# Moebius and attention rounds: the order in which the groups of tiles join and leave

## The chip, the cores and the metric

One core of a Trainium2 chip runs the whole program. The metric is the device time of one execution in microseconds (us); "before" is the median of three runs. A profiled execution is a little longer than these and gives the trace.

## The reference, cut to what matters

Four graph layers run one after the other on 6250 nodes with 128 features and 106250 edges (100000 random ones and a loop on every node): a SAGE layer with two convolutions, a Moebius (hyperbolic) aggregation, an equivariant convolution, and a graph attention. The change lies in the second and the fourth, and in how both order the nodes.

The Moebius layer folds a node's messages one after the other, because `mobius_add` isn't associative:

```python
messages = mobius_add(x[src], -x[dst])
def body(out, em):
    m, idx = em
    return (out.at[idx].set(mobius_add(out[idx], m)), None)
total, _ = jax.lax.scan(body, out0, (messages, dst))
```

The attention layer takes for each node a softmax over its incoming edges, per head, of `leaky_relu(a_src + a_dst + a_edge)`, and the weighted sum of the sources' projected rows; then come a bias and two layer norms with a residual.

## The kernel before, in words

The 6250 nodes stand in 49 tiles of 128, sorted by falling degree (in-edges), so that tile 0 holds the nodes with the most edges. The ranks are worked out on VectorE in the second SAGE sweep (function of that stage, step `k == PLACED`, line 1270), and the rows of the nodes are scattered to HBM in that order.

In the Moebius and the attention stage every partition holds one node of a tile, and each round gives every active tile one more edge. A *half-turn* is one such round; a *turn* is two (`r` = 0, 1), with two halves of the buffer `rows`, so that the gathers of one half-turn run beside the arithmetic of the other. The tiles are in eight groups of `SIZES = (1, 4, 4, 8, 10, 9, 7, 6)`; group 0 is the tile of highest degree. All 49 tiles start together, and the groups leave from the last to the first when their largest degree is used up: `phases` (line 1470) gives, for p = 7 down to 0, the turns in which the groups 0 to p are active. `plan_span` (line 1402) works out the numbers of turns on VectorE from the degrees and writes them to `turns`; all engines load them into registers (`turn_counts`, `turns_before`) and loop over them (`Fori`). Every phase has a loop body of its own in the code of each engine.

A half-turn in the Moebius stage:

- POOL issues one indirect gather per active tile (L1585), 128 rows of `x1_tab` into `rows`. It waits for the indices (`idx_ready`), and before each group until ScalarE has read that group's rows of two half-turns ago (`scaled_ready`).
- ScalarE copies each chunk of up to four tiles to PSUM when its group has landed (L1622), makes the indices of two half-turns later (L1624), waits for the factors `gm` (L1784) and scales each tile's rows (L1633).
- VectorE multiplies each chunk (L1744) and adds it up (L1736), runs some 40 small operations on one number per node (L1755, the mask of nodes with edges left, to L1794), and folds each tile (L1799). When all turns are done it plans the next span (L1434, L1435 and on, L1405 to L1424).

A half-turn in the attention stage: POOL gathers (L2535) when the run of ten tiles has been consumed two half-turns ago; ScalarE makes indices (L2598) and exponentials (L2602); VectorE makes the mask (L2633), the scores (L2636 to L2645), and for each run rescales, weights and adds (L2662, L2665, L2654). When a group of the last five has left, `finish` (L2681 to L2739 on VectorE, with square roots and normalisations on ScalarE) makes the output rows of its tiles; group 3 and the joint groups 0 to 2 are finished together at the end. POOL scatters the output (L2520), 49 in all: 32 after the last gather, then it waits for all engines, SyncE clears the semaphores, POOL reloads a span (L1449, L2545, L1455), and the last 17 scatters follow.

The lines that say in which order tiles are worked on:

```python
PART = tuple(slice(UPTO[g] - SIZES[g], UPTO[g]) for g in range(NG))
def phases(turns):
    for p in reversed(range(NG)):
        yield p, turns[p + 1] if p + 1 < NG else 0, turns[p]
...
        FINISH = [(g, 0, PART[g]) for g in range(NG - 1, 2, -1)] + [(0, 1, slice(0, UPTO[2]))]
        INSIDE = NG - 4
```

## Time and profile before

| | us |
|---|---|
| time before, median of 3 runs | 6176.32 (6172.39 to 6184.4) |
| profiled execution, its own time | 6204.05 |
| its span | 6202.3 |
| POOL busy | 4463.9 (72%) |
| VectorE (DVE) busy | 3342.5 (54%) |
| Moebius rounds, first gather to the plan | 2409.7 to 3616.5 |
| attention, first gather to the end of the span | 4981.0 to 6202.3 |

Times in the trace count from the start of the span. "Busy" is the time in which an engine runs instructions; a row of a group of instructions has the line, the engine, the operation, what it writes and reads, the count, busy us, mean ns of one, and then the engine's idle time just before them with what ended it. "Issue" there is idle time for which the profile shows no wait.

### The profile page before, as it was taken

Reading aid. Unit: us, or ns where it says so; the run is one execution under the profiler, and the core shown is the slowest. Engines: PE = TensorE matmul, PEld = TensorE weight load, DVE = VectorE, ACT = ScalarE, POOL = GpSimd, SP = SyncE. Lnnn points to the kernel's source line nnn. Section 1 sums busy time; section 2 is a strip of 40 time slices with the busy share of each in tenths; the row PEclk is TensorE's granted clock in tenths of the full one; section 3 lists DMA queues with packets and bytes.
Section 4 is the critical chain, followed back from the end, with each engine's and each line's share of the span. In section 5 each row is a group of like instructions: output and inputs, shape, how many; then the busy total and the mean of one; then the engine's idle time right before and its main releaser. Section 6 shows DMA issues by size and latency. Waiting matters only on the chain. (4 is left out here: it accounts for less than half of the span.)

```text
span 6202.3 us, 54339 instructions
## 1 busy us (share of the span) xinstructions
PE 2518.5 (41%) x12736; PEld 1802.9 (29%) x12736; DVE 3342.5 (54%) x8895; ACT 1718.2 (28%) x5753; POOL 4463.9 (72%) x4570
## 2 busy tenths in 40 slices
PE   6888877567776673000000024656666400000000
PEld 4666656455544452000000012334444300000000
DVE  3333333433444355878778875655555524343666
ACT  1111111211111110333333256777777400000111
POOL 6777777577777766777777437777777777777775
PEclk8777676777899875555555567888788755555555
DMA  4333333866666633222222114333333332222221
GB/s 113 119 116 119 116 118 114 208 210 189 191 188 187 179 94 95 54 54 54 54 54 54 34 47 115 101 112 111 110 111 112 105 98 56 55 56 56 56 53 41
DMA packets 404899, 637.29 MB, mean 103 GB/s; under 512 B 148580, under 2 KB 248966, under 8 KB 404340
## 3 DMA queue, kind: packets, MB, share of 16 engines
q0 software_dynamic: 175664, 424.09, 24.4%
q1 hardware_dynamic: 133028, 112.92, 6.7%
q10 hardware_dynamic: 95904, 96.94, 4.8%
q8 instruction: 105, 1.72, 0.1%
q14 instruction: 198, 1.62, 0.1%
HBM read 529.65 MB, written 103.93 MB: 102 GB/s over the span
## 5 line engine op out<-in xcount | busy, mean ns | idle before, releaser
L1585 POOL DMA_INDIRECT mb_rows<-x_tab,mb_idx x882 | 835.5, 947 | 367.2 <-issue 269.8
L2535 POOL DMA_INDIRECT gt_rows<-h_tab,gt_idx x882 | 842.1, 955 | 307.1 <-issue 273.9
L973 POOL DMA_INDIRECT s_rows<-y_split,srcS x824 | 839.3, 1019 | 292.9 <-issue 233.1
L2035 POOL DMA_INDIRECT eq_ring<-fx_tab,srcS x824 | 834.4, 1013 | 262.3 <-issue 248.2
L555 POOL DMA_INDIRECT s_rows<-in_x,srcS x824 | 784.2, 952 | 273.7 <-issue 247.7
L2070 ACT ACTIVATE eq_ring<-eq_ring 128x64 f32<-128x64 f32 x3328 | 814.5, 333 | 338.6 <-DVE eq_ring L2231 310.7
L2111 PE MATMUL eq_ps<-eq_ring,eq_onehot 128*128 128x320 f32 x1664 | 655.6, 552 | 473.5 <-DVE eq_ring L2231 253.0
L2111 PEld LDWEIGHTS eq_ps<-eq_ring,eq_onehot 128*128 128x128 f32 x1664 | 385.3, 242 | 720.3 <-issue 658.6
L1054 PE MATMUL s_ps<-s_onehot,s_rows 128*128 128x128 bf16 x4992 | 452.0, 247 | 310.0 <-DMA s_rows<-y_split,srcS 300.8
L1695 PE MATMUL mb_ps<-ident,mb_rows 128*128 128x128 f32 x49 | 13.6, 331 | 1282.6 <-ACT mb_rows L1662 1281.3
L629 PE MATMUL s_ps<-s_onehot,s_rows 128*128 128x128 f32 x1664 | 459.7, 393 | 159.6 <-DMA s_rows<-in_x,srcS 152.8
L1054 PEld LDWEIGHTS s_ps<-s_onehot,s_rows 128*128 128x128 bf16 x4992 | 355.7, 112 | 431.5 <-DMA s_rows<-y_split,srcS 394.4
L194 DVE TENSOR_TENSOR s_onehot<-iota,dstM 128x512 bf16<-128x512 f32 x206 | 143.2, 696 | 600.6 <-PE s_ps L1054 599.8
L629 PEld LDWEIGHTS s_ps<-s_onehot,s_rows 128*128 128x128 f32 x1664 | 352.5, 254 | 268.8 <-DMA s_rows<-in_x,srcS 215.3
L1744 DVE TENSOR_TENSOR mb_prod<-mb_ps,mb_xf 128x256 f32<-128x256 f32 (+3 forms) x278 | 274.7, 996 | 209.5 <-ACT mb_ps L1622 177.0
L1695 PEld LDWEIGHTS mb_ps<-ident,mb_rows 128*128 128x128 f32 x49 | 6.8, 145 | 1289.9 <-issue 1280.3
L2228 DVE TENSOR_TENSOR eq_ring<-eq_ring 128x512 f32<-128x512 f32 x208 | 143.6, 691 | 439.4 <-DMA eq_ring<-fx_tab,srcS 428.6
L1633 ACT ACTIVATE mb_ps<-mb_rows,mb_gm 128x128 f32<-128x128 f32 x882 | 260.1, 351 | 324.0 <-DVE mb_gm L1784 324.0
L194 DVE TENSOR_TENSOR s_onehot<-s_ps,dstM 128x512 f32<-128x512 f32 x206 | 142.3, 691 | 289.9 <-PE s_ps L630 289.8
L2636 DVE TENSOR_TENSOR span_src<-gt_rows,edges_in 128x196 f32<-128x196 f32 (+7 forms) x36 | 9.4, 261 | 505.7 <-DMA gt_rows<-h_tab,gt_idx 504.4
L1736 DVE TENSOR_REDUCE mb_both<-mb_prod 128x2 f32<-128x256 f32 (+3 forms) x278 | 272.6, 988 | 0.3
L1622 ACT COPY mb_ps<-mb_rows 128x128 f32<-128x128 f32 (+3 forms) x278 | 128.0, 494 | 494.1 <-DMA mb_rows<-x_tab,mb_idx 449.8
(503 smaller groups left out, 5693.9 us busy)
## 6 DMA issues: line engine op xcount, KB each, us to landing
w_tab<-s_wrow ACTq DMA_DIRECT2D x208, 264.0 KB
eq_ring<-w_tab SPq DMA_DIRECT2D x208, 264.0 KB, 2.7
s_es<-in_side ACTq DMA_DIRECT2D x208, 136.0 KB
mb_rows<-x_tab,mb_idx POOLq DMA_INDIRECT x882, 2.5
gt_rows<-h_tab,gt_idx POOLq DMA_INDIRECT x882, 2.5
s_rows<-in_x,srcS POOLq DMA_INDIRECT x824
s_rows<-y_split,srcS POOLq DMA_INDIRECT x824
eq_ring<-fx_tab,srcS POOLq DMA_INDIRECT x824
```

Source lines behind the costliest of these rows:

```text
L194: return dve.tensor_tensor(onehot[:, 4 * half:4 * half + 4], broadcast(numbers, four, 1), broadcast(columns, four, 2), ALU.is_equal)
L555: pool.indirect_dma_start(rows[:, n % SLOTS, :], None, a["x"], bass.IndirectOffsetOnAxis(ap=s["srcS"][:, n:n + 1], axis=0)).then_inc(gathe ...
L629: pe.matmul(ps[:, bank, 0:P], rows[:, slot], onehot[:, u], start=(u == 0), stop=(u == U - 1))
L973: pool.indirect_dma_start(rows[:, n % SLOTS, :], None, t["ys"], bass.IndirectOffsetOnAxis(ap=s["srcS"][:, n:n + 1], axis=0)).then_inc(gath ...
L1054: last = pe.matmul(ps[:, 2 * bank + f, 0:P], rows[:, slot, at:at + P], onehot[:, u], start=(u == 0 and part == 0), stop=(u == U - 1 and pa ...
L1585: pool.indirect_dma_start(rows[:, r, n, :], None, t["x1"], bass.IndirectOffsetOnAxis(ap=idx[:, r, n:n + 1], axis=0)).then_inc(gathered[r][ ...
L1736: do.put(dve.tensor_reduce(both[:, :, lo:hi], prod[:, c % 3, :, 0:hi - lo], AX_X, ALU.add))
L1744: dve.tensor_tensor(prod[:, c % 3, :, 0:hi - lo], copied(c).unsqueeze(1).broadcast_to(wide), xf[:, :, lo:hi, 0:D], ALU.mult).then_inc(mult ...
L2035: pool.indirect_dma_start(frow[:, n % SLOTS, :], None, features, bass.IndirectOffsetOnAxis(ap=s["srcS"][:, n:n + 1], axis=0)).then_inc(gat ...
L2070: last = act.activation(pb[:, r % 2, u, f].rearrange("p c w -> p (c w)"), wrow[:, r, u, lo:lo + 64], ACT.Copy, scale=wrow[:, r, u, D + f:D ...
L2111: last = pe.matmul(ps[:, bank, 0:MC], onehot[:, 4 * h + u], msg[:, h, u], start=(h == 0 and u == 0), stop=(h == 1 and u == 3))
L2535: pool.indirect_dma_start(rows[:, r, n, :], None, flat, bass.IndirectOffsetOnAxis(ap=idx[:, r, n:n + 1], axis=0)).then_inc(gathered[r][g], 16)
```

## The change

The tiles are laid out anew: the 27 tiles of groups 0 to 4 stand in rising order of degree (group 4 first, group 0 last), then groups 5, 6, 7. The ranks get three more operations that reverse the first 27 x 128. The rounds begin with groups 0 to 4 alone. When group 4 (ten tiles) has ended, groups 5, 6 and 7 (22 tiles) join with their first edges, and the groups leave in the order 4, 3, 2, 1, 7, 6, 5, 0. So the active tiles are always adjacent (`WINDOW`). Because the joined groups count their turns from the joining, masks, index columns and semaphore values use two counts, `e` and `e + turns[0]` (`group_turn`), and operations on a column of edges are made once for each of up to two windows. In the attention stage the runs of ten tiles become six unequal stretches, every group is finished when it leaves, and 48 of the 49 scatters come ahead of the reload.

```diff
 WTILES = 2 * BODIES * WB
 NT = TILES + 1
 SPAN = 48
+SRCS = SPAN + 15
 READY = tuple(-(-(G * P * (g + 1) * E // N + 700) // EB) for g in range(GROUPS - 1))
 SIZES = (1, 4, 4, 8, 10, 9, 7, 6)
 NG = len(SIZES)
-UPTO = tuple(sum(SIZES[:g + 1]) for g in range(NG))
-PART = tuple(slice(UPTO[g] - SIZES[g], UPTO[g]) for g in range(NG))
-CHUNKS = tuple((g, n, min(n + 4, UPTO[g])) for g in range(NG) for n in range(PART[g].start, PART[g].stop, 4))
-CHUNKS_TO = tuple(sum(1 for c in CHUNKS if c[0] <= g) for g in range(NG))
+FIRST = 5
+PLACES = (*reversed(range(FIRST)), *range(FIRST, NG))
+PART = tuple(slice(sum(SIZES[x] for x in PLACES[:PLACES.index(g)]), sum(SIZES[x] for x in PLACES[:PLACES.index(g) + 1]))
+             for g in range(NG))
+HEAD = PART[FIRST].start
+LEAVE = (4, 3, 2, 1, 7, 6, 5, 0)
+TURN = (0, 5, 6, 7, 1, 2, 3, 4)
+ACTIVE = tuple(tuple(g for g in TURN if LEAVE.index(g) >= p and (p or g < FIRST)) for p in range(NG))
+WINDOW = tuple((min(PART[g].start for g in on), max(PART[g].stop for g in on)) for on in ACTIVE)
+CHUNKS = tuple((g, n, min(n + 4, PART[g].stop)) for g in TURN for n in range(PART[g].start, PART[g].stop, 4))
+CHUNKS_TO = {g: max(k for k, c in enumerate(CHUNKS) if c[0] == g) + 1 for g in range(NG)}
+ON = tuple(tuple(k for k, c in enumerate(CHUNKS) if c[0] in on) for on in ACTIVE)
 WW = D + 4
...
                 if k == PLACED:
+                    do(dve.tensor_scalar(key, rank[:], -2.0, float(HEAD * P - 1), ALU.mult, ALU.add))
+                    do(dve.scalar_tensor_tensor(key, rank[:], float(HEAD * P), key, ALU.is_lt, ALU.mult))
+                    do(dve.tensor_tensor(rank[:], rank[:], key, ALU.add))
                     do(dve.tensor_copy(s["rank"][:], rank[:]))
...
-    for g in range(NG):
-        do.put(dve.tensor_reduce(q[:, 0, g:g + 1], s["tile_max"][:, PART[g]], AX_X, ALU.max))
+    for j, g in enumerate(LEAVE):
+        do.put(dve.tensor_reduce(q[:, 0, j:j + 1], s["tile_max"][:, PART[g]], AX_X, ALU.max))
     do.sync()
...
-    for g in range(NG - 2, -1, -1):
-        do(dve.scalar_tensor_tensor(q[:, 1, g:g + 1], q[:, 1, g + 1:g + 2], 1.0, q[:, 1, g:g + 1], ALU.add, ALU.max))
+    do(dve.tensor_scalar(q[:, 1, 4:7], q[:, 1, 4:7], q[:, 1, 0:1], None, ALU.add))
+    for j in range(1, NG):
+        do(dve.scalar_tensor_tensor(q[:, 1, j:j + 1], q[:, 1, j - 1:j], 1.0, q[:, 1, j:j + 1], ALU.add, ALU.max))
     do(dve.tensor_tensor(q[:, 2, 0:NG], q[:, 2, 0:NG], q[:, 3, 0:NG], ALU.add))
     do.put(dve.tensor_copy(s["turns"][:, 1, 0:NG], q[:, 2, 0:NG]))
     do.put(dve.tensor_copy(s["turns"][:, 0, 0:NG], q[:, 1, 0:NG]))
     do(dve.tensor_copy(q[:, 3, 0:NG], q[:, 1, 0:NG]))
-
-
-PLAN_OPS = 5 + NG + 6 + (NG - 1) + 4
+    do.put(dve.tensor_scalar(q[:, 3, 4:7], q[:, 1, 4:7], q[:, 1, 0:1], None, ALU.subtract))
+    do(dve.tensor_scalar(s["turns"][:, 0, 1:NG], q[:, 1, 1:NG], q[:, 1, 0:1], None, ALU.subtract))
+
+
+PLAN_OPS = 5 + NG + 7 + (NG - 1) + 6
...
 def phases(turns):
-    for p in reversed(range(NG)):
-        yield p, turns[p + 1] if p + 1 < NG else 0, turns[p]
+    for p in range(NG):
+        yield p, turns[p - 1] if p > 1 else 0, turns[p]
 
 
 def turn_counts(eng, s):
 
-    return [eng.value_load(s["turns"][0:1, 0, g:g + 1], min_val=1, max_val=SPAN // 2 + NG - 1) for g in range(NG)]
+    return [eng.value_load(s["turns"][0:1, 0, p:p + 1], min_val=1, max_val=SPAN // 2 + NG - 1) for p in range(NG)]
 
 
 def turns_before(eng, s):
 
-    return [eng.value_load(s["turns"][0:1, 1, g:g + 1], min_val=0, max_val=65535 // (16 * SIZES[g]) - 2 * SPAN) for g in range(NG)]
+    return [eng.value_load(s["turns"][0:1, 1, LEAVE.index(g):LEAVE.index(g) + 1], min_val=0,
+                           max_val=65535 // (16 * SIZES[g]) - 2 * SPAN) for g in range(NG)]
+
+
+def group_turn(p, g, e, turns):
+    return e + turns[0] if p and g < FIRST else e
+
+
+def windows(p):
+    lo, hi = WINDOW[p]
+    return [(0, lo, HEAD)] if hi <= HEAD else [(0, lo, HEAD), (FIRST, HEAD, hi)]
+
+
+def source_column(s, lo, hi, k):
+    return s["span_all"][:, bass.ds(k + lo * SRCS, (hi - lo) * SRCS)].rearrange("p (t k) -> p t k", k=SRCS)[:, :, 0]
 
...
             with pool.Fori(0, span_count(pool, s)) as c:
-                for p, lo, hi in phases(turn_counts(pool, s)):
-                    with pool.Fori(lo, hi) as b:
+                turns = turn_counts(pool, s)
+                for p, lo, hi in phases(turns):
+                    with pool.Fori(lo, hi) as e:
+                        b = group_turn(p, 0, e, turns)
                         for r in range(2):
                             pool.wait_ge(idx_ready[r], b + 1)
                             pool.sem_inc(took, 1)
-                            for g in range(p + 1):
+                            for g in ACTIVE[p]:
...
+                                act.copy(copied(i, hi_ - lo_), rows[:, r, lo_:hi_, 0:D]).then_inc(copied_ready, after(p, i) - k)
+                            for first, lo_, hi_ in windows(p):
+                                ins = act.copy(idx[:, r, lo_:hi_],
+                                               source_column(s, lo_, hi_, group_turn(p, first, e, turns) * 2 + (2 + r)))
+                            ins.then_inc(idx_ready[r], 1)
...
-                            for k in range(CHUNKS_TO[p]):
+                            for i, k in enumerate(ON[p]):
                                 g, lo_, hi_ = CHUNKS[k]
-                                if k >= 4:
...
-            def turn(p, b, r):
-                T = UPTO[p]
-                many = CHUNKS_TO[p]
+            def turn(turns, p, e, b, r):
+                at, to = WINDOW[p]
+                T, many = to - at, len(ON[p])
                 dve.sem_clear(own)
...
                         dve.wait_ge(own, c - 2)
                     wide = [P, 2, hi - lo, D]
-                    dve.tensor_tensor(prod[:, c % 3, :, 0:hi - lo], copied(c).unsqueeze(1).broadcast_to(wide), xf[:, :, lo:hi, 0:D],
...
-                xs2, y2 = rows[:, r, 0:T, D], xd[:, 0:T, D]
-                dve.tensor_scalar(valid, s["span_deg"][:, 0:T], s["iota"][:, bass.ds(2 * b + r, 1)], None, ALU.is_gt)
...
+                xs2, y2 = rows[:, r, at:to, D], xd[:, at:to, D]
+                for first, lo, hi in windows(p):
+                    dve.tensor_scalar(w[5][:, lo:hi], s["span_deg"][:, lo:hi],
+                                      s["iota"][:, bass.ds(group_turn(p, first, e, turns) * 2 + r, 1)], None, ALU.is_gt)
                 dve.tensor_scalar(t0, dt, -2.0, 1.0, ALU.mult, ALU.add)
...
-        column = lambda T, k, f: edges_in[:, bass.ds(k, T * SPAN)].rearrange("p (t j) f -> p t j f", j=SPAN)[:, :, 0, f]
+        column = lambda lo, hi, k, f: edges_in[:, bass.ds(k + lo * SPAN, (hi - lo) * SPAN)].rearrange(
+            "p (t j) f -> p t j f", j=SPAN)[:, :, 0, f]
         bias, gain, shift = (sb(n, [P, D]) for n in ("bias", "gain", "shift"))
         idx = sb("idx", [P, 2, TILES], I32)
         MOST = max(SIZES)
-        RUN = 10
-        RUNS = -(-TILES // RUN)
-        FINISH = [(g, 0, PART[g]) for g in range(NG - 1, 2, -1)] + [(0, 1, slice(0, UPTO[2]))]
-        INSIDE = NG - 4
+        STRETCHES = ((26, 36), (36, 43), (43, 49), (18, 26), (10, 18), (0, 10))
+        RUNS = len(STRETCHES)
+        run_of = lambda n: next(c for c, (lo, hi) in enumerate(STRETCHES) if lo <= n < hi)
+        own_run = lambda p, c, e, turns: group_turn(p, 0 if STRETCHES[c][0] < HEAD else FIRST, e, turns)
+        runs_of = lambda p: [(c, max(lo, WINDOW[p][0]), min(hi, WINDOW[p][1])) for c, (lo, hi) in enumerate(STRETCHES)
+                             if lo < WINDOW[p][1] and hi > WINDOW[p][0]]
+        FINISH = [(g, 0, PART[g]) for g in LEAVE]
         stats, mv = sb("stats", [P, 2, MOST, 6]), sb("mv", [P, 2, MOST, 2])
...
                         for r in range(2):
                             pool.wait_ge(idx_ready[r], b + 1)
                             pool.sem_inc(took, 1)
-                            for g in range(p + 1):
+                            opened = set()
+                            for g in ACTIVE[p]:
                                 for n in range(PART[g].start, PART[g].stop):
-                                    if n % RUN == 0:
-                                        pool.wait_ge(consumed[r][n // RUN], b + 1)
+                                    if run_of(n) not in opened:
+                                        opened.add(run_of(n))
+                                        pool.wait_ge(consumed[r][run_of(n)], own_run(p, run_of(n), e, turns) + 1)
                                         pool.sem_inc(took, 1)
                                     pool.indirect_dma_start(rows[:, r, n, :], None, flat,
                                                             bass.IndirectOffsetOnAxis(ap=idx[:, r, n:n + 1], axis=0)
                                                             ).then_inc(gathered[r][g], 16)
-                for k in range(INSIDE):
+                for k in range(NG - 1):
                     pool.wait_ge(normed[0], 2 * k + 2)
                     scatter(FINISH[k][2])
...
                 pool.sem_inc(src_ready, 1)
-                for k in range(INSIDE, len(FINISH)):
-                    scatter(FINISH[k][2])
+                scatter(FINISH[NG - 1][2])
                 pool.wait_ge(scattered, 16 * TILES)
...
+                    with dve.Fori(lo, hi) as e:
+                        b = group_turn(p, 0, e, turns)
                         for r in range(2):
-                            turn(before, p, b, r)
-                    if NG - 1 - p < INSIDE:
-                        finish(NG - 1 - p)
-                finish(INSIDE, INSIDE + 1)
+                            turn(turns, before, p, e, b, r)
+                    finish(p)
```

## Rows read from the trace of the kernel before

**Rows 1.** Page, part 1, and POOL's busy tenths of 40 slices (part 2)

```profile
PE 2518.5 (41%) x12736; PEld 1802.9 (29%) x12736; DVE 3342.5 (54%) x8895; ACT 1718.2 (28%) x5753; POOL 4463.9 (72%) x4570
...
POOL 6777777577777766777777437777777777777775
```

**Rows 2.** Page, part 5 (Moebius gathers) and part 6 (attention's, us to landing)

```profile
L1585 POOL DMA_INDIRECT mb_rows<-x_tab,mb_idx x882 | 835.5, 947 | 367.2 <-issue 269.8
...
gt_rows<-h_tab,gt_idx POOLq DMA_INDIRECT x882, 2.5
```

**Rows 3.** Waits of the Moebius stage: us in total, times, longest

```profile
POOL mb_rows L1585 <- ACT mb_ps L1633: 70.8, 22, 9.3
...
POOL mb_rows L1585 <- ACT mb_idx L1624: 26.6, 5, 7.4
...
DVE mb_prod L1744 <- issue: 24.2, 5, 5.0
```

**Rows 4.** Timeline of the Moebius stage, first gather and planning

```profile
2409.68 0.99 POOL L1585 DMA_INDIRECT mb_rows<-x_tab,mb_idx  x1 [9.38 <-issue]
...
3616.52 0.15 DVE L1434 TENSOR_SCALAR base<-base 128x1 f32<-128x1 f32 x1 [0.32 <-DVE mb_xf L1799]
```

**Rows 5.** Groups of VectorE's instructions by shape, Moebius stage, line L1755

```profile
L1755 DVE TENSOR_SCALAR mb_w<-span_deg,iota 128x49 f32<-128x49 f32 x12 | 3.0, 249 | 1.9 <-DVE mb_both L1736 1.9
...
L1755 DVE TENSOR_SCALAR mb_w<-span_deg,iota 128x1 f32<-128x1 f32 x10 | 2.1, 214 | 1.6 <-DVE mb_both L1736 1.6
...
L1755 DVE TENSOR_SCALAR mb_w<-span_deg,iota 128x5 f32<-128x5 f32 x4 | 1.1, 282 | 0.6 <-DVE mb_both L1736 0.6
...
L1755 DVE TENSOR_SCALAR mb_w<-span_deg,iota 128x43 f32<-128x43 f32 x2 | 0.5, 244 | 0.3 <-DVE mb_both L1736 0.3
```

**Rows 6.** Windows from mask to mask, Moebius: length, busy PE, PEld, DVE, ACT, POOL

```profile
2539.02:2600.26 61.24, 0.00 (x0) 0.00 (x0) 48.62 (x117) 21.68 (x65) 46.30 (x50) 0.50 0.21 55
...
3386.84:3420.60 33.76, 0.00 (x0) 0.00 (x0) 28.72 (x82) 11.88 (x36) 25.53 (x28) 0.50 0.21 55
...
3445.18:3466.22 21.04, 0.00 (x0) 0.00 (x0) 19.75 (x66) 7.52 (x23) 15.13 (x16) 0.50 0.21 55
...
3466.22:3483.01 16.79, 0.00 (x0) 0.00 (x0) 15.17 (x61) 6.41 (x21) 8.51 (x9) 0.50 0.13 33
...
3483.01:3496.82 13.81, 0.00 (x0) 0.00 (x0) 12.52 (x54) 4.07 (x13) 4.74 (x5) 0.50 0.12 29
...
3539.89:3548.39 8.50, 0.00 (x0) 0.00 (x0) 6.78 (x46) 1.85 (x7) 0.95 (x1) 0.50 0.04 8
...
3576.31:3583.03 6.72, 0.00 (x0) 0.00 (x0) 5.38 (x42) 0.68 (x3) 0.95 (x1) 0.50 0.01 2
```

**Rows 7.** Windows, attention: half-turn of 49 tiles, finish of 10, half-turn of 17

```profile
5628.26:5689.09 60.83, 0.00 (x0) 0.00 (x0) 24.95 (x30) 2.07 (x3) 46.07 (x49) 0.50 0.22 56
...
6005.96:6029.86 23.90, 0.00 (x0) 0.00 (x0) 19.51 (x65) 5.96 (x16) 18.11 (x20) 0.50 0.22 57
...
6042.90:6053.87 10.97, 0.00 (x0) 0.00 (x0) 9.92 (x20) 0.51 (x2) 8.32 (x9) 0.50 0.22 58
```

**Rows 8.** Waits of the attention stage, POOL's own

```profile
POOL gt_rows L2535 <- DVE gt_ps L2665: 25.4, 9, 7.3
...
POOL gt_rows L2535 <- ACT gt_idx L2598: 7.7, 3, 2.6
```

**Rows 9.** Timeline of the attention stage, its start and its end

```profile
4980.96 0.99 POOL L2535 DMA_INDIRECT gt_rows<-h_tab,gt_idx  x1 [8.92 <-issue]
...
5001.03 6.82 POOL L2535 DMA_INDIRECT gt_rows<-h_tab,gt_idx  x1 [0.30 <-issue]
...
6169.46 0.15 DVE L1424 COPY plan_q<-plan_q 1x8 f32<-1x8 f32 x1
...
6178.34 0.99 POOL L2520 DMA_INDIRECT out<-gt_rows,perm  x1 [1.05 <-issue]
...
6198.62 0.96 POOL L2520 DMA_INDIRECT out<-gt_rows,perm  x1 [0.30 <-issue]
```

More of the change, by code:

```diff
@@ L1635, in _ @@
+                                ins.then_inc(scaled_ready, after(p, i) - k)
                 act.sem_inc(arrived, 1)
@@ L1743, in turn @@
                     wide = [P, 2, hi - lo, D]
[L1744 to L1745 removed]
+                    dve.tensor_tensor(prod[:, c % 3, :, 0:hi - lo], copied(c, hi - lo).unsqueeze(1).broadcast_to(wide), xf[:, :, lo:hi, 0:D],
+                                      ALU.mult).then_inc(multiplied, after(p, c) - k)
                     if c:
@@ L1806, in _ @@
                 for p, lo, hi in phases(turns):
-                    with dve.Fori(lo, hi) as b:
+                    with dve.Fori(lo, hi) as e:
+                        b = group_turn(p, 0, e, turns)
                         for r in range(2):
-                            turn(p, b, r)
+                            turn(turns, p, e, b, r)
                 do = Chain(dve, plan_own, c * NEXT_OPS)
@@ L2524, in _ @@
             with pool.Fori(0, span_count(pool, s)) as c:
-                for p, lo, hi in phases(turn_counts(pool, s)):
-                    with pool.Fori(lo, hi) as b:
+                turns = turn_counts(pool, s)
+                for p, lo, hi in phases(turns):
+                    with pool.Fori(lo, hi) as e:
+                        b = group_turn(p, 0, e, turns)
                         for r in range(2):
@@ L2622, in _, with turn @@
             by_head = "p u (h c) -> p u h c"
-            def turn(before, p, b, r):
-                T = UPTO[p]
+            def turn(turns, before, p, e, b, r):
+                at, to = WINDOW[p]
+                T = to - at
                 four = [P, T, heads]
-                aek = column(T, 2 * b + r, slice(0, heads))
-                al, sc, dn, old, new = alpha[:, 0:T], scores[:, 0:T], den[:, 0:T], top[:, 1 - r, 0:T], top[:, r, 0:T]
-                adst = own_row[:, 0:T, D + heads:HW]
-                valid4 = valid[:, 0:T].unsqueeze(2).broadcast_to(four)
+                al, sc, dn, old, new = alpha[:, at:to], scores[:, at:to], den[:, at:to], top[:, 1 - r, at:to], top[:, r, at:to]
+                adst = own_row[:, at:to, D + heads:HW]
+                valid4 = valid[:, at:to].unsqueeze(2).broadcast_to(four)
@@ L2631, in turn @@
                 dve.sem_clear(turn_own)
                 do = Chain(dve, turn_own)
-                dve.tensor_scalar(valid[:, 0:T], s["span_deg"][:, 0:T], s["iota"][:, bass.ds(2 * b + r, 1)], None, ALU.is_gt)
-                for g in range(p + 1):
-                    dve.wait_ge(gathered[r][g], (before[g] + b + 1) * (16 * SIZES[g]))
-                do(dve.tensor_tensor(al, rows[:, r, 0:T, D:D + heads], aek, ALU.add))
-                dve.tensor_scalar(limit_[:, 0:T], valid[:, 0:T], 2.0 * BIG, -BIG, ALU.mult, ALU.add)
+                spans = windows(p)
@@ new lines, in turn @@
+                for first, lo, hi in spans:
+                    dve.tensor_scalar(valid[:, lo:hi], s["span_deg"][:, lo:hi],
+                                      s["iota"][:, bass.ds(group_turn(p, first, e, turns) * 2 + r, 1)], None, ALU.is_gt)
+                for g in ACTIVE[p]:
+                    dve.wait_ge(gathered[r][g], (group_turn(p, g, e, turns) + before[g] + 1) * (16 * SIZES[g]))
+                aek = [column(lo, hi, group_turn(p, first, e, turns) * 2 + r, slice(0, heads)) for first, lo, hi in spans]
@@ L2640, in turn @@
                 do(dve.scalar_tensor_tensor(al, al, NEG, al, ALU.mult, ALU.max))
-                do(dve.tensor_tensor(sc, al, limit_[:, 0:T].unsqueeze(2).broadcast_to(four), ALU.min))
+                do(dve.tensor_tensor(sc, al, limit_[:, at:to].unsqueeze(2).broadcast_to(four), ALU.min))
                 do(dve.tensor_tensor(new, sc, old, ALU.max))
-                dve.tensor_tensor(below[:, 0, 0:T], old, new, ALU.subtract)
-                dve.tensor_tensor(below[:, 1, 0:T], sc, new, ALU.subtract).then_inc(below_ready, 1)
@@ L2649, in turn @@
-                runs = [(c, c * RUN, min(c * RUN + RUN, T)) for c in range(-(-T // RUN))]
-                weights = lambda c, many: ps[:, 1 + 3 * (c % 2):4 + 3 * (c % 2), :].rearrange("p b n -> p (b n)")[:, 0:many * D]
-                def add_up(c, lo, hi):
-                    dve.wait_ge(consumed[r][c], b + 2)
-                    do.put(dve.tensor_tensor(acc[:, lo:hi], weights(c, hi - lo).rearrange("p (u d) -> p u d", d=D),
+                dve.tensor_tensor(dn, dn, ex[:, 0, at:to], ALU.mult)
@@ new lines, in turn, with add_up @@
+                do(dve.tensor_tensor(ex[:, 1, at:to], ex[:, 1, at:to], valid4, ALU.mult))
+                runs = [(i, c, lo, hi) for i, (c, lo, hi) in enumerate(runs_of(p))]
+                weights = lambda i, many: ps[:, 1 + 3 * (i % 2):4 + 3 * (i % 2), :].rearrange("p b n -> p (b n)")[:, 0:many * D]
+                def add_up(i, c, lo, hi):
+                    dve.wait_ge(consumed[r][c], own_run(p, c, e, turns) + 2)
+                    do.put(dve.tensor_tensor(acc[:, lo:hi], weights(i, hi - lo).rearrange("p (u d) -> p u d", d=D),
@@ L2655, in add_up @@
                                              acc[:, lo:hi], ALU.add))
-                    added[c] = do.n
+                    added[i] = do.n
                 added = {}
-                for c, lo, hi in runs:
+                for i, c, lo, hi in runs:
                     wide = [P, hi - lo, heads, cols]
```

127 lines of the change are left out of this document (65 added, 62 removed).

## The prediction

> **What bounds the kernel now.** I read the page first, then the groups of instructions with their shapes, windows cut at half-turns, the two lists of waits, and the timeline where the two stages begin and end. The reader is to see in the page that POOL is busy for 72% of the span, more than any other engine, and that its busy share falls twice while work is still left: in the 23rd and 24th slice, and in the last [rows 1]. The first dip is the tail of the Moebius stage, the second that of the attention stage. Both stages are long rows of indirect gathers, 882 each; one takes 947 ns and the engine then sits 0.305 us on "issue" (269.8 us in the 855 cases that are no other wait, 9.4 of them ahead of the first) [rows 2, 3, 4]. So a gather costs 1.252 us, and 882 of them cost 1104.3 us in each stage, however they are ordered.
>
> How the gathers are spread is in the shapes of L1755, one per half-turn: 12 half-turns on 49 tiles, two each on 43, 36, 27, 17 and 9 (the rows of 36, 27, 17 and 9 read like that of 43), four on 5 and ten on 1 [rows 5]. That is 36 half-turns, 18 turns, and says when each group ends: group 7 after 6 turns, then 7, 8, 9, 10, 11, 13 and 18 for group 0. The windows show two regimes [rows 6]. With 49 tiles a half-turn takes 61.24 us, which is 49 x 1.252 = 61.3: gathers set it, and VectorE is busy for 48.62. With 27 tiles it takes 33.76 (27 x 1.252 = 33.8), VectorE busy 28.72; with 17, 21.04 (21.3). Below that VectorE sets it: 13.81 with 9 tiles where the gathers need 11.3, 6.72 with one where they need 1.25. So POOL waits there: 70.8 + 26.6 us in 27 waits, of which 27 x 0.305 is the usual issue time, which leaves 89.2 us [rows 3]. The account closes: 2409.7 + 1104.3 + 89.2 is 3603.2, and the planning that follows the last half-turn begins at 3616.5 [rows 4].
>
> Attention is the same with less VectorE work: with 49 tiles the half-turn is 60.83 us and VectorE is busy for 24.95 [rows 7]. POOL's waits there are 25.4 + 7.7 us in 12 cases, so 29.4, and one gather takes 6.82 instead of 0.95 [rows 8, 9]; together 35.3 beyond 1104.3, so the last slot ends at 4981.0 + 1139.6 = 6120.6.
>
> **The change part by part.** *Turns.* Groups 0 to 4 (27 tiles) run first, nine turns, until group 4 ends; then groups 5, 6, 7 join with 8, 7 and 6 turns of their own and end at turns 17, 16 and 15, group 0 at 18. From the ends above the active tiles by turn are 27 (nine times), 39, 31, 27, 27, 23, 23, 17, 10, 1. Twice their sum, 441, is 882: not one gather less, and the same 36 half-turns. What moves is where they lie: only the last four half-turns (10, 10, 1, 1) are below 17 tiles, against 16 before.
>
> *Moebius.* I let POOL set every half-turn of 17 tiles or more, as the windows of 27 and 17 do. Those are 860 gathers, from 2409.7 to 2409.7 + 860 x 1.252 = 3486.4. The old second half-turn of 17 has its gathers issued by 2409.7 + 834 x 1.252 = 3453.9 and begins its small operations at 3466.2, 12.3 us later [rows 6]; the new one comes behind 23 tiles instead of 27, and VectorE is less behind, so I take 11: 3497.4. From there VectorE sets the pace: 17 to 10 tiles 17.2 (16.79 for 17 to 9, plus one tile at about 0.4), 10 to 10 14.7 (13.81 plus 0.9), 10 to 1 10.5 (between 8.50 for 5 to 1 and 13.81), 1 to 1 6.7, and at most 6.7 for the last: 55.8, end at 3553.2. POOL's waits would fall from 89 to about 26 us. Gain 3616.5 - 3553.2 = 63.3.
>
> *Added operations, Moebius.* A second mask operation in the 16 half-turns of two windows, three more in the plan, and a second copy of indices on ScalarE: about 0.2 us each (the mask takes 244 ns on 43 tiles, 214 on one [rows 5]). In POOL's regime they lie under gathers (VectorE idles 5.04 of 33.76 us); in the last half-turns and the plan they cost about 1.6, or 4 if that cover were gone throughout. The three operations that reverse the ranks run in the sweep before, which also waits on gathers: nothing, or 0.7. I take 1.6 in all: 61.7 left.
>
> *Loop jumps.* VectorE waits for nothing that the profile shows ahead of a product in five places, 24.2 us in all [rows 3]. Five is the number of jumps back in the loop of 49 tiles (six turns); a jump costs 4.8 there and is hidden by the gathers. The new kernel jumps back ten times in bodies of 27 and 23 tiles. The small loops don't show the wait, so the price lies between nothing and 4.8; I take it as paid and hidden, because a turn of 27 tiles leaves VectorE 2 x 5.04 us idle. Uncovered, ten jumps cost up to 48 us; that is a rival below. The Trainium skill (Runtime: NRT & Kernel Launch, section "Instruction fetch mechanics") says that a taken branch whose target is outside the current two pages must fetch it first; these five rows fit that. By that page the smaller body may or may not stay within; the sum stays as it is either way, since the idle time covers it.
>
> *Attention, gathers.* Everything down to 10 tiles is set by gathers: VectorE needs 10.97 us for 17 tiles against 21.3 [rows 7]. The finish of a group now comes after each phase (eight instead of four and one joint one); 10 tiles take 23.90 us [rows 7], hidden while the next two half-turns' gathers last longer (up to 97 us). It shows only after group 6: the gathers of the last 17-tile half-turn end at 4980.96 + 860 x 1.252 + 5.9 = 6063.6, their data is there 1.3 later (2.5 from issue [rows 2] less the slot), VectorE needs 11.0 and the finish of 7 tiles about 19 (16.7 by proportion to 23.9 at the most): 6094.9. The 10-tile half-turn frees its first tiles some 6.6 us later (an estimate: three fifths of the 10.97), 6101.5, where the gathers of both 10-tile half-turns have been out since 6088.6. So the first 1-tile gather waits 13, the second 6, and the last slot ends at 6110.3. Before it was 6120.6: 10.3 won.
>
> *Attention, scatters.* Before, 32 tiles are written after the gathers, then POOL waits until VectorE has finished the last 17 (plan ends at 6169.46), and 8.9 us later it writes these [rows 9]. Now 48 tiles go out first, at (6198.62 - 6178.34)/16 = 1.267 us, until 6110.3 + 60.8 = 6171.1; VectorE, with 9 tiles and 1 tile to finish, two half-turns and the plan, is through by some 6150, so it is under the scatters. Then 8.9 us as before, one scatter at 6180.0, and 3.7 us to the end as from 6198.62 to 6202.3: 6183.7. Attention wins 18.6 in all. If the finish of six tiles, one phase earlier, came into the open as well (14.3 us by proportion to 23.9), nearly all of that would be lost.
>
> *Sum.* 61.7 + 18.6 = 80.3 of a span of 6202.3: 6122. Its own time, 6204.05, lies 1.75 above the span and 0.45% above the median of the runs shown, 6176.32. So 6123.8 / 6204.05 = 0.9871, times 6176.32: **6096 us**.
>
> **Rivals.** *(a) Half-turns of 27 are too tight.* 22 of 36 half-turns now have 27 tiles, and there VectorE is at 28.72 of 33.76, where 49 tiles leave it 12.6. If the jumps are not covered, ten of them at 4.8 give 6144. Against it: two half-turns hold 10.1 us of idle time per jump.
>
> *(b) Attention wins nothing.* More finishes, each with its two rounds over ScalarE, fall on POOL's path, or the wait for group 5's finish comes back ahead of the scatters. Then only Moebius counts: 6114. For it: the wait before the 1-tile gathers is as large as all waits that go.
>
> *(c) Slower.* POOL checks a semaphore ahead of each group or stretch of tiles, and all these values become sums of two registers. By the order of the code there are 164 such waits in Moebius (as many as before), 126 in attention (104 before) and 72 for indices: 362. Today a half-turn of 49 gathers takes 49 times a gather, so they are hidden. If they came to stand in the open, the gain would be gone at 80.3/362 = 0.22 us each; at 0.3, what one issue takes, the time is 6205. It decides only if the arithmetic no longer fits under a gather.
>
> *(d) The change doesn't do what it says*: more turns than 18. Group 5 ends at 9 + 8 = 17 turns and 18 remains group 0's, so a whole turn is spare; time 6176 if it took one turn per group more. The rows nearly exclude it.
>
> **How the numbers follow.** Forecast 0.77, (a) 0.08, (b) 0.09, (c) 0.04, (d) 0.02. The forecast's own bounds: Moebius waits of 16 to 40 us instead of 26 and the finish of group 6 at 16.7 to 23.9 give 6083 to 6117. The range from 6078 to 6126 takes (b) in and leaves (a), (c) and (d) out. Within 0.2% (12 us, about what a measurement of this kernel tells from no change) is (d) and a little of (a); slower by over 0.2% is (c). Faster 0.93, same 0.03, slower 0.04.
>
> **What would show it.** The mask of Moebius with 18 half-turns on 27 tiles (and 27 again later) at 33.8 us, 39 at 48.8; POOL's waits in Moebius near 26 instead of 89 us, all in the last four half-turns; the stage from its first gather to the plan near 1145 us instead of 1207. In attention a wait near 13 us ahead of the last two gathers, 48 scatters without a gap, and less than 10 us between them and the last one. The forecast is wrong if 27-tile half-turns take 35 or more, if a gather takes more than 1.26 us on average, or if VectorE's finish stops POOL earlier than in the last phase.

## The result, and the profile after

The changed kernel takes **6089.53 us** (median, 6080.92 to 6097.74), the kernel before on the same chip 6174.35: a ratio of 0.986, 95% interval 0.984 to 0.9879. Faster by 1.4%, and 6.5 us under the predicted 6096. On another chip the same pair gave 6111.2 and 6200.27, ratio 0.9858 (0.9843 to 0.9873). The medians of the kernel before differ by 26 us between the chips of this study, so the ratios are compared, and stages within one profile.

Busy time of the engines, and POOL's tenths over 40 slices (page, parts 1 and 2), to be held against [rows 1]:

```profile
PE 2548.4 (42%) x12736; PEld 1822.2 (30%) x12736; DVE 3367.4 (55%) x9090; ACT 1736.3 (29%) x5802; POOL 4433.6 (73%) x4570
...
POOL 5777777577777775777777737777777777777776
```

The dip in the last slices of Moebius has shrunk to one digit, which holds the change of stages; the last digit has risen from 5 to 6. Moebius: timeline of its start and end, and POOL's waits (us in total, times, longest), against [rows 3, 4]:

```profile
2401.96 0.99 POOL L1618 DMA_INDIRECT mb_rows<-x_tab,mb_idx  x1 [9.38 <-issue]
...
3540.95 0.15 DVE L1450 TENSOR_SCALAR base<-base 128x1 f32<-128x1 f32 x1 [0.33 <-DVE mb_xf L1836]
```

```profile
POOL mb_rows L1618 <- issue: 275.1, 873, 9.4
POOL mb_rows L1618 <- ACT mb_ps L1667: 23.5, 9, 14.0
```

The stage now takes 1139.0 us, from 1206.8: **67.9 us won**. Gathers are 882 as before; the waits for ScalarE went from 70.8 + 26.6 us in 27 cases to 23.5 in nine, which less the usual 0.3 of each is 20.8. These 20.8 lie ahead of four gathers, 871, 872, 881 and 882, all in the last four half-turns. Before, 89.2 us lay ahead of 15 gathers, from 844 on.

Windows of single half-turns with 27, 39, 23, 17 (the second), then 17 to 10, 10 to 10, 10 to 1 and 1 to 1 tiles (columns as in [rows 6]):

```profile
2546.19:2579.97 33.78, 0.00 (x0) 0.00 (x0) 28.71 (x82) 11.87 (x36) 25.56 (x28) 0.50 0.24 54
3066.25:3115.05 48.80, 0.00 (x0) 0.00 (x0) 39.67 (x103) 17.49 (x53) 36.91 (x40) 0.50 0.25 54
3383.85:3412.52 28.67, 0.00 (x0) 0.00 (x0) 25.36 (x79) 10.36 (x33) 21.66 (x24) 0.50 0.25 54
3464.90:3486.15 21.25, 0.00 (x0) 0.00 (x0) 19.97 (x70) 7.70 (x25) 16.07 (x18) 0.50 0.25 55
3486.15:3503.73 17.58, 0.00 (x0) 0.00 (x0) 15.97 (x66) 6.69 (x23) 10.48 (x12) 0.50 0.18 43
3503.73:3518.67 14.94, 0.00 (x0) 0.00 (x0) 13.64 (x59) 4.66 (x16) 2.25 (x3) 0.50 0.07 16
3518.67:3528.75 10.08, 0.00 (x0) 0.00 (x0) 8.36 (x52) 3.31 (x12) 0.94 (x1) 0.50 0.04 8
3528.75:3535.46 6.71, 0.00 (x0) 0.00 (x0) 5.38 (x42) 0.68 (x3) 0.00 (x0) 0.50 0.00 0
```

Down to 17 tiles the length is the number of tiles times 1.25; only the last rows lie above it. Attention: first gather, the last two gathers with their waits, and the end (timeline of POOL), against [rows 9]:

```profile
4891.32 0.99 POOL L2581 DMA_INDIRECT gt_rows<-h_tab,gt_idx  x1 [9.02 <-issue]
...
6012.96 0.94 POOL L2581 DMA_INDIRECT gt_rows<-h_tab,gt_idx  x1 [14.13 <-DVE gt_ps L2717]
6020.50 0.94 POOL L2581 DMA_INDIRECT gt_rows<-h_tab,gt_idx  x1 [6.60 <-DVE gt_ps L2717]
6021.74 0.99 POOL L2562 DMA_INDIRECT out<-gt_rows,perm  x1 [0.30 <-issue]
...
6081.84 0.95 POOL L2562 DMA_INDIRECT out<-gt_rows,perm  x1 [0.30 <-issue]
6082.80 0.20 POOL L1465 COPY reload_at<-span_at 128x1 int32 x1
6083.83 1.01 POOL L2591 DMA_INDIRECT gt_again<-edge_tab,reload_at  x1 [0.83 <-POOL reload_at L1465]
6086.89 0.38 POOL L1471 COPY edges_in<-gt_again 128x240 f32 x1 [2.05 <-DMA gt_again<-edge_tab,reload_at]
6088.30 0.99 POOL L2562 DMA_INDIRECT out<-gt_rows,perm  x1 [1.03 <-issue]
```

From the first gather to the end of the span (6091.7) it is 1200.4 us, from 1221.3: **20.9 won**. Half of it lies in the gathers (first to last 10.1 us shorter), half behind them. The reload copy follows the 48th scatter at once, with no wait for SyncE.

The two stages give 88.8 us of the 6202.3, or 1.43%; the ratio says 1.40. What else differs between the two profiles (the stretch from the plan of Moebius to the first gather of attention is 1364.4 before and 1350.4 here) is not of the change, as the first experiment and the runs behind it show together.

### The profile page after: what moved, and what is told of

It is laid out like the page before. It is cut to its first block and busy times, and to the rows that moved or that the text cites. A ratio compares the mean times of both kernels' runs of the same rounds, so it can differ in the third digit from the quotient of the medians.

```text
span 6091.7 us, 54710 instructions
## 1 busy us (share of the span) xinstructions
PE 2548.4 (42%) x12736; PEld 1822.2 (30%) x12736; DVE 3367.4 (55%) x9090; ACT 1736.3 (29%) x5802; POOL 4433.6 (73%) x4570
## 3 DMA queue, kind: packets, MB, share of 16 engines
q14 instruction: 174, 1.43, 0.1%
## 5 line engine op out<-in xcount | busy, mean ns | idle before, releaser
L983 POOL DMA_INDIRECT s_rows<-y_split,srcS x824 | 825.8, 1002 | 297.0 <-issue 238.2
L2073 POOL DMA_INDIRECT eq_ring<-fx_tab,srcS x824 | 819.8, 995 | 262.7 <-issue 248.4
L1779 DVE TENSOR_TENSOR mb_prod<-mb_ps,mb_xf 128x1024 f32<-128x1024 f32 (+3 forms) x278 | 274.0, 996 | 139.4 <-ACT mb_ps L1656 117.7
L1771 DVE TENSOR_REDUCE mb_both<-mb_prod 128x8 f32<-128x1024 f32 (+3 forms) x278 | 271.9, 988 | 0.1
L1836 DVE SCALAR_TENSOR_TENSOR mb_xf<-mb_xf,mb_v,mb_ps 128x128 f32<-128x128 f32 x882 | 244.3, 342 | 14.3 <-DVE mb_n L1831 4.1
```

What stands on the lines that cost most here:

```text
L983: pool.indirect_dma_start(rows[:, n % SLOTS, :], None, t["ys"], bass.IndirectOffsetOnAxis(ap=s["srcS"][:, n:n + 1], axis=0)).then_inc(gath ...
L1771: do.put(dve.tensor_reduce(both[:, :, lo:hi], prod[:, c % 3, :, 0:hi - lo], AX_X, ALU.add))
L1779: dve.tensor_tensor(prod[:, c % 3, :, 0:hi - lo], copied(c, hi - lo).unsqueeze(1).broadcast_to(wide), xf[:, :, lo:hi, 0:D], ALU.mult).then ...
L2073: pool.indirect_dma_start(frow[:, n % SLOTS, :], None, features, bass.IndirectOffsetOnAxis(ap=s["srcS"][:, n:n + 1], axis=0)).then_inc(gat ...
```

## The experiments

Stage lengths below are read as above, from the first gather to the plan (Moebius) and from the first gather to the end of the last recorded instruction (attention; 1218.6 before and 1198.0 after by this reading). Each ratio is to the kernel before on the same chip.

**The kernel before, once more.** No edit.

> The kernel before, unchanged, profiled once more. In the two profiles of the pair the second SAGE sweep differed by 14.1 us (1097.3 before, 1083.2 after) and the equivariant stage by 13.9 (1138.8, 1124.9), although no loop of theirs was changed. Theory: this is spread from one execution to the next, and the profiled execution of before was 28 us above its median for this reason; so another profile of before shows at least one of the two stages more than 5 us shorter. Rival: the change made them shorter (another layout of the buffers, other code); then both stand at 1097 and 1139 again, within 3. In either case Moebius is 1206 to 1208 us from its first gather to the plan.

Moebius 1206.5, attention 1218.4, and the stretch between them 1364.1 us: the same as in the first profile. So that profile alone speaks for the rival. But the runs below, which have the changed kernel's code in that stretch, show 1359.9 to 1368.3 us there, and a second profile of the changed kernel 1361.7. Up to the first gather of Moebius it is 2405.2 us here, and 2392 to 2411 in those runs. So the differences were one execution's, and the expectation that before would show the shorter one too was wrong.

**The old order in the new layout.** Group lists, windows and chunks are made by a function, for one order or the other; sums with `turns[0]` and the three plan operations are neutral in the old order.

```diff
-LEAVE = (4, 3, 2, 1, 7, 6, 5, 0)
...
+    LEAVE = (4, 3, 2, 1, 7, 6, 5, 0) if joined else (7, 6, 5, 4, 3, 2, 1, 0)
...
+        use_order(False)
         sage(nc, a, t, s)
         moebius(nc, a, t, s)
+        use_order(False)
...
-    return e + turns[0] if p and g < FIRST else e
+    return e + turns[0] if JOINED and p and g < FIRST else e
```

> The new layout, masks, windows, stretches and scatters, but the old order: all 49 tiles start together and the groups leave as before, 7 first and 0 last, in both stages. Theory (the gain is POOL's idle time in half-turns below 17 tiles, filled by the order): Moebius is 1205 to 1210 us long again with POOL's waits near 90 us, and the time is near 6170; up to 10 less for the 48 scatters ahead of the reload, up to 25 more because groups 3, 2 and 1 are now finished one by one between short half-turns. Rival (the gain comes from the new code and layout, such as smaller steps or cheaper operations): 6090 to 6110.

6234.79 us (6221.43 to 6240.34) against 6195.96: ratio 1.0068 (1.0051 to 1.0084), **slower than before**. Moebius is 1204.1 us with waits 89.1 above the usual: the theory's numbers, so code and layout win nothing there, and the rival (6090 to 6110) falls. Moebius is 0.9 us below the expected 1205 to 1210, and the step from gather to gather was 1.249 us in this execution, where it was 1.252 before. POOL's waits in Moebius:

```profile
POOL mb_rows L1626 <- ACT mb_ps L1675: 69.3, 17, 9.3
POOL mb_rows L1626 <- ACT mb_idx L1666: 26.6, 5, 7.4
```

Attention is 1253.7, 35 us more than before, and beyond what I expected. Waits of POOL in attention:

```profile
POOL gt_rows L2589 <- DVE gt_ps L2725: 74.5, 12, 20.3
...
POOL gt_rows L2589 <- ACT gt_idx L2653: 7.8, 3, 2.6
```

Before there were 25.4 + 7.7 [rows 8]. Three of the waits here, of 20.32, 14.18 and 18.19 us, stand ahead of gathers 853, 863 and 875 of the 882, the first ones of turns 12, 13 and 15. One turn earlier groups 3, 2 and 1 have left: VectorE then runs that group's finish, and only the half-turn behind it frees the rows. Before, these groups were finished at the end. Above the usual 0.3 of each, the waits grew by 48 us (77.7 against 29.4); 35 is what is left of it, because the 48 scatters give back some 10 us behind the last gather (68.1 us to the end, before 78.4) and the shorter step 2.

**The new order in one stage alone.** The two kernels take the new order for Moebius, or for attention, and the old one as above for the other stage.

> The new order in Moebius alone; attention has the old order with the new layout. Theory: Moebius 1139 us, 66 to 68 us less than in the run with the old order in both stages, so about 6103 (6095 to 6135, by what attention is there). Rival (the gain is not additive, an earlier end of Moebius is lost again later): less than 55 us less.

6170.42 (6166.44 to 6175.6), ratio 0.9963 (0.995 to 0.9975). Moebius 1140.1 us, attention 1255.4. POOL's waits in Moebius:

```profile
POOL mb_rows L1626 <- ACT mb_ps L1675: 24.1, 11, 14.0
```

Against the old order in both stages that is 64.4 us less, and Moebius alone is 64.0 less, 2 below the expected 66 to 68 and well over the rival's 55. The waits fell as in the first pair (89.1 to 20.8 here, 89.2 to 20.8 there). But the step was 1.251 us in this profile and 1.249 in that of the old order, which over 881 steps takes 1.9 us back. Why the step differs between executions, by up to 3 ns and with either order, no run shows. The absolute time came 67 us over the expected 6103, mostly because I did not foresee the 35 us of attention, and because this chip is slower (before: 6195.96 against 6174.35).

> The new order in attention alone; Moebius has the old order. Theory: attention 1200 us from its first gather to the end as with the whole change, Moebius 1207, so the time is that of the changed kernel and 67 us: 6156. That is 18 to 21 us less than before. Rival (attention wins nothing by its order and the rest is spread): 6168 to 6176.

6179.22 (6165.56 to 6183.66), ratio 0.997 (0.996 to 0.998). Moebius 1206.0, attention 1198.1. So 16.7 us won (12 to 25 by the interval), a little less than the 18 to 21 of the theory. The absolute time is above the theory's 6156 and the rival's 6168 to 6176, because these were set from the faster chip; against the kernel before, the rival allows at most 8 us, and it falls. This ratio times Moebius' share (67.9 of 6204, or 0.9891) is 0.9861: the two stages add up.

**The finish of before.** Moebius in the new order; attention in the old one, with four groups finished when they leave, the rest at the end, and 32 scatters ahead of the reload.

```diff
-        FINISH = [(g, 0, PART[g]) for g in LEAVE]
+        FINISH = [(g, 0, PART[g]) for g in LEAVE[:5]] + [(0, 1, slice(PART[2].start, PART[0].stop))]
+        INSIDE = 4
...
-                    finish(p)
+                    if p < INSIDE:
+                        finish(p)
+                finish(INSIDE, INSIDE + 1)
```

> The new order in Moebius; attention with the old order and the finish of before: four groups when they leave, group 3 and the joint groups 0 to 2 at the end, 32 scatters ahead of the reload. In the run with the old order and a finish for every group, attention was 35 us longer than before (1253.7 against 1218.6), with waits of 21.3, 15.1 and 19.1 us ahead of gathers. Theory (these waits are the finishes of groups 4, 3 and 2 or 1 between short half-turns; layout, windows and stretches cost nothing): attention 1216 to 1222 us. Rival (the new layout's stretches or its second operations cost it): above 1235.

6123.59, ratio 0.9893 (0.9878 to 0.9908). Attention 1215.1 us, just under the expected 1216 to 1222: layout, stretches and windows cost nothing. The edit takes back the finishes and the scatters together. So the waits tell what the finishes between short half-turns cost, some 49 us (those of groups 3, 2 and 1, as the order of the waits shows, not 4 as I wrote):

```profile
POOL gt_rows L2590 <- DVE gt_ps L2730: 29.3, 11, 5.3
```

**32 scatters ahead of the reload, 17 behind it.**

```diff
-                for k in range(NG - 1):
+                for k in range(5):
...
-                scatter(FINISH[NG - 1][2])
+                for k in range(5, NG):
+                    scatter(FINISH[k][2])
```

> The changed kernel, but only 32 tiles are scattered ahead of the reload and 17 behind it, as before the change. Theory (the 10.5 us won behind the last gather come from VectorE being through earlier, not from where the reload stands): the pause at the reload moves behind the 32nd scatter and is 5 to 9 us instead of 5.2, so attention is 1198 to 1202 us. Rival (the split itself wins it, because 48 queued scatters hide SyncE's hand-over): the pause is 15 us again, attention 1208.

6114.82 (6103.35 to 6116.06), ratio 0.9883 (0.9868 to 0.9898). Timeline of POOL at the pause:

```profile
6062.80 1.58 POOL L2562 DMA_INDIRECT out<-gt_rows,perm  x1 [0.30 <-issue]
6072.28 0.18 POOL L1465 COPY reload_at<-span_at 128x1 int32 x1 [7.90 <-SPq L2553]
6073.32 1.02 POOL L2591 DMA_INDIRECT gt_again<-edge_tab,reload_at  x1 [0.85 <-POOL reload_at L1465]
6076.31 0.38 POOL L1471 COPY edges_in<-gt_again 128x240 f32 x1 [1.98 <-DMA gt_again<-edge_tab,reload_at]
6077.74 0.99 POOL L2562 DMA_INDIRECT out<-gt_rows,perm  x1 [1.05 <-issue]
```

VectorE's plan ends at 6068.88, so POOL waits for it and then for SyncE. From one scatter's start to the next it is 14.94 us: the rival's number, and my theory falls, although attention (1203.4) lies between the two. Behind its last gather this kernel needs 75.6 us, the changed one 67.9, before 78.4. So of the 10.5 us some 7.7 come from the 48 scatters, under which VectorE's plan and SyncE's hand-over go on, and 2.8 from the rest of the change, the order and the finish of each group; no run parts these two. The old order with 48 scatters needs 68.1 there: with 48 the order no longer matters.

**Three microseconds more of VectorE in every half-turn of Moebius.**

```diff
                 dve.sem_inc(took, 1)
+                do(dve.memset(extra[:], 0.0))
```

> The changed kernel with one more VectorE instruction at the end of every Moebius half-turn: a fill of 128x3560 that nothing reads, about 3.0 us by the fill of 128x6272 in 5.29 us. Theory (in half-turns of 27 tiles VectorE has about 5 us to spare): 27 tiles stay at 33.7 us, and only the half-turns of 17, 10 and 1 tiles at the end grow, 5 or 6 of them: Moebius 1154 to 1158 us instead of 1139. Rival (27 tiles are at the edge, as rival (a) of the prediction says): all 36 half-turns grow by 2 to 3 us, Moebius 1210 or more.

6144.21 (6142.34 to 6154.35), ratio 0.9934 (0.9918 to 0.9951). The fill takes 3025 ns; Moebius grows to 1182.0 us, by 43 or 44, between the two expectations. Windows: 17 half-turns of 27 tiles together, then one of 23, the second of 17, 17 to 10, and 10 to 10:

```profile
2444.60:3026.70 582.10, 0.00 (x0) 0.00 (x0) 539.14 (x1396) 202.99 (x612) 440.09 (x467) 0.50 0.21 54
...
3395.28:3426.58 31.30, 0.00 (x0) 0.00 (x0) 28.55 (x80) 10.50 (x33) 23.68 (x26) 0.50 0.21 54
3484.76:3509.75 24.99, 0.00 (x0) 0.00 (x0) 22.89 (x71) 7.78 (x25) 10.19 (x11) 0.50 0.13 32
3509.75:3531.07 21.32, 0.00 (x0) 0.00 (x0) 18.90 (x66) 6.70 (x23) 9.43 (x10) 0.50 0.12 32
3531.07:3549.82 18.75, 0.00 (x0) 0.00 (x0) 16.64 (x60) 4.65 (x16) 0.94 (x1) 0.50 0.02 4
```

Where VectorE sets the pace, a half-turn grew by 3.7 to 3.8 (17.58 to 21.32, 14.94 to 18.75): the fill and the wait for its end. With 27 tiles a half-turn is 34.24 on average (582.10/17), half a microsecond longer than in the changed kernel (573.60/17 = 33.74), and VectorE now sets its own pace: it has no wait for ScalarE's copies in that stretch. Less 3.8 that is an estimate of 30.4 us for VectorE's own half-turn of 27 tiles: **3.3 us to spare, not the 5.04 that its idle time suggests**, since some of that is waits of its own. By the same sum 23 tiles have 1.2 to spare (31.30 - 3.8 = 27.5 against 28.7) and 17 tiles nothing (21.2 against 21.25). That bounds this order: the turn of 17 stands at the edge.

The 43 us, though, do not lie in the half-turns of 27 tiles. Up to gather 827 of the 882 POOL never waits more than the usual 0.3 us. With two halves of `rows`, VectorE can fall behind by half a microsecond in each half-turn without stopping POOL, and a half-turn of 39 tiles gives some of it back (46.08 us, where the changed kernel's took 48.80, set by the gathers). POOL's waits:

```profile
POOL mb_rows L1619 <- ACT mb_ps L1668: 64.1, 36, 17.8
```

Above the usual 0.3 of each wait that is 53.2 us, from 20.8, all ahead of the last 55 gathers. From the last gather to the plan it is 28.5 us, from 17.0. Together that is 44 us, less 1 for a shorter step.

**A longer loop body.** 25 or 50 fills of one element (59 ns each) at the end of each half-turn of the first phase, so 267 or 317 instructions of VectorE in the records of that body instead of 217.

> The changed kernel with 25 more VectorE fills of one element at the end of each half-turn of the first 27 tiles, so that this loop body has about 267 instructions in the records instead of 217. Theory (the 3 to 4 us that a jump back cost in the body of 49 tiles, with 327 to 329 instructions, come from the length of the body): between 0.25 and 4 us per jump; where it starts is what this run tells. Rival (they come from something else in the half-turn of 49 tiles): 0.25 us.

> As e8a_longer25 with 50 fills per half-turn, about 317 instructions in the body. Theory (length): a jump back costs 2.5 us or more in the loop of 27 tiles. Rival: 0.25 us, as at 217 instructions.

6118.26 and 6117.1 us (one run each), Moebius 1140.2 and 1140.3. A jump back, read from the end of VectorE's branch instruction to the next record of that engine, takes 0.23 to 0.28 us in both, as in the changed kernel; the waits of VectorE have no row on "issue" ahead of a product in that stretch. In the old order's 49 tiles, with 329 instructions, the row is there, in the new code too, and the jump takes 2.9 to 3.0:

```profile
DVE mb_prod L1787 <- issue: 17.5, 5, 3.6
```

So up to 317 recorded instructions the theory of length is not borne out. Whether the step lies between 317 and 327, or something else in the half-turn of 49 tiles makes it, stays open: records are not all instructions. The row alone does not tell a jump: the changed kernel has it too (20.6 us in six cases), but 12.5 of that stand ahead of the first product, and the other five cases lie between two chunks of a half-turn, none at a jump.

**A step on: join one phase later.** Groups 5 to 7 join when group 3 has ended, groups 5 and 0 end together, and the 1-tile turn is gone.

```diff
-ACTIVE = tuple(tuple(g for g in TURN if LEAVE.index(g) >= p and (p or g < FIRST)) for p in range(NG))
+JOIN = 2
+PHASES = NG - 1
+ACTIVE = tuple(tuple(g for g in TURN if LEAVE.index(g) >= p and (p >= JOIN or g < FIRST)) for p in range(PHASES))
...
     for j in range(1, NG):
+        if j == JOIN:
+            do(dve.tensor_scalar(q[:, 1, 4:7], q[:, 1, 4:7], q[:, 1, JOIN - 1:JOIN], None, ALU.add))
...
+    do(dve.tensor_copy(q[:, 1, 6:7], q[:, 1, 7:8]))
...
-    return e + turns[0] if p and g < FIRST else e
+    return e + turns[JOIN - 1] if p >= JOIN and g < FIRST else e
...
+                finish(PHASES)
```

> A step on from the changed kernel: groups 5, 6, 7 join one phase later, when group 3 (8 tiles) has ended, and groups 5 and 0 end together, so there are seven phases and no turn of one tile. Active tiles by turn: 27 nine times, 17, 31, 27, 27, 23, 23, 23, 17, 10, still 441. Theory (what is left of POOL's idle time is the 1-tile turn): Moebius 6 us shorter (1133: from the last 17 tiles on 47.4 us of half-turns instead of 56, less two gathers), attention about 20 shorter (no wait of 13.8 and 6.3 ahead of the last two gathers), about 26 in all. Rival (the last half-turns of ten tiles leave VectorE two finishes behind the last gather, and POOL waits for them ahead of the scatters): attention wins less than 8.

6083.74 (6070.39 to 6087.5), ratio 0.9827 (0.9812 to 0.9841). Moebius 1127.0 us, 11 to 13 less than the 1138.1 to 1140.3 of the other kernels in the new order; its last half-turn is 8.53 us, and POOL's waits are 6.4 us in five cases. Attention 1185.1, 13 less. Expected were 6 in Moebius and about 20 in attention. There the waits ahead of the last gathers are gone, but one of 5.3 us has come elsewhere, and SyncE's hand-over comes into the open again:

```profile
6071.15 0.95 POOL L2566 DMA_INDIRECT out<-gt_rows,perm  x1 [0.30 <-issue]
6076.75 0.18 POOL L1469 COPY reload_at<-span_at 128x1 int32 x1 [4.65 <-SPq L2557]
```

> The changed kernel once more, to stand beside the kernel that joins one phase later on the same chip. Ratio to before 0.985 to 0.987; Moebius 1138 to 1140 us, attention 1195 to 1201.

> The same kernel as e6_join_later again. Theory (24 to 25 us of it lie in the two stages, 11 in Moebius and 13 in attention, as its profile showed): 20 to 28 us under the changed kernel on the same chip. Rival (the profile of one execution flattered it): less than 12 us under it.

Side by side: 6111.2 (6091.48 to 6115.92; 0.9858, 0.9843 to 0.9873) and 6094.75 (6090.58 to 6101.67; 0.9832, 0.9818 to 0.9845). The medians are 16 us apart, between theory (20 to 28) and rival (under 12), and the intervals just touch. In the profiles Moebius is 1138.1 against 1129.0, attention 1195.1 against 1187.9, which is 16 as well. The step was 1.249 us in the one and 1.251 to 1.252 in the other, which over both stages is 4.6 us; at equal steps the gap would be 21 (an estimate). So it is the best version of the study, by 16 to 24 us, less sure in size than in sign.

## Why the prediction was right

*Mechanism.* POOL's idle time in half-turns of fewer than 17 tiles was the gain in Moebius. To the 67.9 us won the waits gave 68.4 (89.2 to 20.8) and the shorter step of this execution 1.8, while the way from the last gather to the plan grew by 2.5. The old order in the new code brings back 89.1 us of waits and 1204.1 us; the new order in this stage alone takes 64.0 away. Not one gather less, and the step stays about the same: 1.249 to 1.251 us in Moebius with the new code whatever the order, 1.252 before.

*Moebius, sizes.* Predicted 1145 us, measured 1139.0. Three terms were too large. The step was 1.2499 in this execution, not 1.252, which over 860 gathers is 1.8 us. The small operations of the second 17-tile half-turn began 9 us behind its gathers (3486.15 against 2401.96 + 860 x 1.2499 = 3476.9), not 11. And the tail from there was 54.8 us (3540.95 - 3486.15), where I had 55.8 + 1.6. Together they make up the difference. The waits were 20.8, not 26.

*Loop jumps.* Taken as 4.8 us each, paid and hidden. The cover held, but there was nothing to hide: 0.25 us each in the 27-tile loop. The range from nothing to 4.8 was right, the value taken was not. Had they cost 4.8, the 2 x 3.3 us that a turn of 27 tiles has to spare would have covered them, but by less than my 2 x 5.04. The 4.8 was also more than the jump: from the branch to the next record it was 3.8 to 4.1 us there. The page of the Trainium skill that I cited (Runtime: NRT & Kernel Launch, "Instruction fetch mechanics") ties such a stall to a branch target outside the current two pages; the body with 317 recorded instructions does not show a stall, and no run here shows where pages end.

*Attention, gathers.* Predicted 10.3 us with waits of 13 and 6 ahead of the last two gathers; measured 10.1 with 13.8 and 6.3. The last gather before:

```profile
6120.22 0.95 POOL L2535 DMA_INDIRECT gt_rows<-h_tab,gt_idx  x1 [2.13 <-DVE gt_ps L2665]
```

This was the most detailed step, and it held in its parts too: VectorE's half-turn of 17 took 11.0 us as predicted, the finish of seven tiles 18.2 instead of 19, and the first gather came 8.5 us behind it instead of 6.6.

*Attention, end.* Predicted 8.3 us to the end of the span, measured 10.8 (10.5 to the end of the last instruction): 48 scatters without a gap for VectorE, then 5.2 us beyond a slot instead of 8.9 to the last scatter. The step "8.9 us as before" was mis-sized: it held 3.2 us between the end of VectorE's plan (6169.61) and POOL's reload copy, and this hand-over too goes on under the scatters:

```profile
6172.78 0.19 POOL L1449 COPY reload_at<-span_at 128x1 int32 x1 [10.43 <-SPq L2511]
```

*Rivals.* (a) 27-tile half-turns: not too tight, but a third closer to it than I wrote. With 3 us more of VectorE in each, POOL did not wait over nine turns. (b) The finishes on POOL's path are real in the old order: 48 us of waits, 35 of them left in the time. The new order pays for finishing every group on its own, because after groups 4, 3, 2 and 1 there are long half-turns to hide it. I had called this hidden without seeing that the old order would not hide it. (c) The semaphore waits cost nothing that the step shows. (d) The turns are 18.

## What to carry to other kernels

When one engine's work is fixed in amount and only its spread changes, count the stretches in which it is not the bound, and move work from the long ones into the short ones; the total follows from the step and the waits that are left. An edit that costs time alone (a finish for each group) can be right together with an order that covers it, so test the parts in both orders. Idle time of the second engine is not all spare: put in a known delay, and see where the half-turn begins to grow and where the engine that is the bound begins to wait.

## What was not expected of the hardware

48 indirect writes that POOL issues behind each other hid a hand-over between three engines completely: the reload copy at 6082.80 starts as the 48th scatter ends. With 32 queued the same step waits 7.90 us for SyncE.

A jump back of VectorE costs 0.23 to 0.28 us in bodies of 217 to 317 recorded VectorE instructions and 2.9 to 4.1 in those of 327 to 329, and in the latter less with the new code (2.9 to 3.2) than before (3.8 to 4.1). The cause of the difference was not found.
